# Eight row tiles normalised in four steps instead of two, and head 0 in another order

## What is computed

```python
xn = _layernorm(x, axis=-1)                      # mean, variance, eps 1e-5
x = x + _L0_attn_ref(xn, ...) + _L0_ffn_ref(xn, ...)

# attention: 16 heads of 128
q = rmsnorm(xn @ Wq, q_rms_w); k = rmsnorm(xn @ Wk, k_rms_w); v = xn @ Wv
scores = q @ k.T * scale + bias                  # bias = -distance * slope of the head
attn = softmax(where(causal, scores, -inf))
y = rmsnorm(attn @ v, subln_w)
out = y @ Wproj

# ffn: x / s rounded to float8, times s, then times the float8 weight * scale
```

## Time and profile before

| | |
|---|---|
| median of 3 runs | 524.42 us (524.07 to 524.53) |
| the profiled execution: time, span | 524.42 us, 522.5 us |
| TensorE (PE) busy | 508.9 us, 97% |
| VectorE (DVE) busy | 434.0 us, 83% |
| ScalarE (ACT) busy | 376.9 us, 72% |
| GpSimd (POOL) busy | 348.3 us, 67% |

### The profile page before, as it was taken

The page is one execution under the profiler, slowest core; times in us unless marked ns, Lnnn a source line. Parts: engine busy times, 40 slices in busy tenths (PEclk is TensorE's granted clock), DMA queues, the critical chain, the costliest instruction groups (busy, mean ns, idle before and its releaser), DMA issues. The chain is left out here.

```text
span 522.5 us, 11980 instructions
## 1 busy us (share of the span) xinstructions
PE 508.9 (97%) x3348; PEld 467.0 (89%) x3348; DVE 434.0 (83%) x1058; ACT 376.9 (72%) x887; POOL 348.3 (67%) x494
## 2 busy tenths in 40 slices
PE   8998999999999999999999999999999999999986
PEld 4987898999999899999989999998999999999775
DVE  5688789888888888898898888889888887988964
ACT  3678687687868768786776968678696867868650
POOL 5687885866858387783858658584885838667121
PEclk9999999999999999999999999999999999999999
DMA  5200101010010101001010000101000000000002
GB/s 156 72 2 11 31 1 41 3 32 10 2 41 0 40 0 40 0 0 40 0 40 0 21 19 0 40 0 40 0 14 26 0 10 0 11 1 1 3 0 80
DMA packets 18614, 10.82 MB, mean 21 GB/s; under 512 B 2208, under 2 KB 18592, under 8 KB 18592
## 3 DMA queue, kind: packets, MB, share of 16 engines
q1 hardware_dynamic: 17600, 10.49, 6.8%
q10 hardware_dynamic: 992, 0.07, 0.1%
HBM read 9.51 MB, written 1.05 MB: 20 GB/s over the span
## 5 line engine op out<-in xcount | busy, mean ns | idle before, releaser
L863 ACT ACTIVATE stage<-qkv_ps 128x384 f32<-128x384 f32 x116 | 57.1, 492 | 86.5 <-PE qkv_ps L551 86.5
L1110 DVE TENSOR_TENSOR pT_lo<-pT_ps,pT_hi 128x384 fp32r<-128x384 f32 (+2 forms) x192 | 100.6, 552 | 11.9 <-ACT pT_hi L891 11.7
L891 ACT ACTIVATE pT_hi<-pT_ps 128x384 fp32r<-128x384 f32 (+2 forms) x192 | 86.7, 485 | 28.9 <-PE pT_ps L634 28.8
L883 ACT ACTIVATE probs<-probs,neg_max 128x256 f32<-128x256 f32 (+7 forms) x128 | 99.0, 775 | 3.5 <-DVE neg_max L1101 2.7
L634 PE MATMUL pT_ps<-ident,probs 128*128 128x128 f32 x576 | 86.0, 276 | 4.2 <-ACT probs L883 2.9
L549 PE MATMUL qkv_ps<-w_hi,xT_hi 128*128 128x384 f32 x240 | 87.8, 366 | 0.0
L551 PE MATMUL qkv_ps<-w_hi,xT_lo 128*128 128x384 f32 x240 | 81.1, 338 | 0.0
L634 PEld LDWEIGHTS pT_ps<-ident,probs 128*128 128x128 f32 x576 | 66.2, 140 | 16.5 <-issue 5.8
L550 PE MATMUL qkv_ps<-w_lo,xT_hi 128*128 128x384 f32 x240 | 80.8, 336 | 0.0
L423 POOL TENSOR_TENSOR qk_r<-qk_ms,minus_half 128x4 f32<-128x4 f32 x64 | 64.9, 1015 | 17.1 <-DVE qk_ms L1077 15.7
L549 PE MATMUL yT_ps<-pT_hi,v_hi 128*128 128x256 f32 (+1 forms) x224 | 73.1, 326 | 0.4 <-DVE pT_lo L1110 0.4
(11 more groups left out here) (203 smaller groups left out, 1323.3 us busy)
## 6 DMA issues: line engine op xcount, KB each, us to landing
w_raw<-in_wq SPq DMA_DIRECT2D x16, 128.0 KB, 2.2
w_raw<-in_wk SPq DMA_DIRECT2D x16, 128.0 KB, 2.3
w_raw<-in_wv SPq DMA_DIRECT2D x16, 128.0 KB, 2.4
wp_raw<-in_wproj SPq DMA_DIRECT2D x16, 128.0 KB, 2.1
acc<-in_x SPq DMA_DIRECT2D x4, 256.0 KB, 4.9
out<-acc SPq DMA_DIRECT2D x8, 128.0 KB, 1.8
w<-in_ffn_w ACTq DMA_DIRECT2D x1, 64.0 KB, 5.7
q_col<-in_q_w ACTq DMA_DIRECT2D x1, 0.5 KB, 3.0
```

The costliest lines, as they stand in the source:

```text
L863: act.activation(stage_of(h, k // 2)[:, k % 2, :], qkv_bank(h, k)[:, 0:3 * D], ACT.Copy).then_inc(qkv_read, 1)
L883: act.activation(probs[:, s % 2, 0:(i + 1) * P], probs[:, s % 2, 0:(i + 1) * P], ACT.Exp, bias=neg_max[:, par, s:s + 1], scale=-1.0, accum ...
L891: act.activation(pT_hi[g][:, a:b, r * P:(r + 1) * P], pT_ps[(chunk0(h, s) + k) % 2][:, 0:(b - a) * P].rearrange("p (j t) -> p j t", t=P), ...
L1110: dve.tensor_tensor(pT_lo[g][:, a:b, r * P:(r + 1) * P], pT_ps[(chunk0(h, s) + k) % 2][:, 0:(b - a) * P].rearrange("p (j t) -> p j t", t=P ...
```

## The change

Loads: head 0's weights are loaded between the second and the third quarter of x. Prologue: moments, power and normalisation go by two row tiles, in four steps; row tiles 0 to 3 are normalised by ScalarE (`activation` with scale 1/std and a shift of -mean/std that VectorE computes, `shift_x`), row tiles 4 to 7 by VectorE as before. A PSUM bank of `xT_bank` now holds both halves of the channels of two tiles, so `round_xT` and `split_xT` do two whole row tiles each. The low part of head 0's weights is made in two pieces with a semaphore each. The warm-up has 16 products, and 2 behind each of the first two groups of transposes instead of 10 behind the first four tiles. Head 0: the same calls in another order on TensorE, ScalarE, VectorE and GpSimd. The FFN weights' transposes come before those of the last row tile. The number of bytes loaded and every product of the attention and the FFN are the same.

```diff
@@ on SP
-            for n in range(4):
+            def load_x(n):
                 quarter = slice(n * NT // 4, (n + 1) * NT // 4)
                 sp.dma_start(acc[:, quarter, :], x_v[:, quarter, :]).then_inc(x_loaded[n], 16)
...
+            load_x(0)
+            load_x(1)
             load_w(0, 0)
+            load_x(2)
+            load_x(3)
             load_w(1, 1)
             load_wp(0, 0)
@@ on GpSimd
-            for n in range(2):
-                at = slice(n * NT // 2, (n + 1) * NT // 2)
-                if n == 1:
-                    pool.wait_ge(w_hi_done, 1)
-                    pool.tensor_tensor(w_lo[:, 0], w_raw[:, 0], w_hi[:, 0].bitcast(f32), ALU.subtract).then_inc(w_split, 1)
+            def root_x(n):
+                at = slice(n * NT // 4, (n + 1) * NT // 4)
                 pool.wait_ge(var_ready, n + 1)
                 pool.tensor_tensor(rstd[:, at], rstd[:, at], minus_half[:, at], ALU.pow).then_inc(rstd_ready, 1)
+            def low_w(kt):
+                pool.wait_ge(w_hi_done, 1)
+                pool.tensor_tensor(w_lo[:, 0, kt], w_raw[:, 0, kt], w_hi[:, 0, kt].bitcast(f32),
+                                   ALU.subtract).then_inc(w_half if kt == 0 else w_split, 1)
...
-            pool.wait_ge(w_split, 1)
+            root_x(0)
+            root_x(1)
+            low_w(0)
+            low_w(1)
+            root_x(2)
+            root_x(3)
             pool.wait_ge(xn_ready, NT)
             split_w(1, 1)
             norm_qk(0, 0)
             norm_qk(0, 1)
             norm_qk(0, 2)
             norm_qk(0, 3)
+            norm_qk(1, 0)
             split_v(0, 0, 0)
             split_v(0, 0, 1)
-            norm_qk(1, 0)
             pool.wait_ge(small_loaded, 80)
             pool.wait_ge(xT_read, 2 * KT)
+            split_w(2, 0)
             split_v(0, 0, 2)
             split_v(0, 0, 3)
-            split_w(2, 0)
@@ on TensorE
-                    if isinstance(h, int) and h == 0 and k % 4 == 0:
-                        pe.wait_ge(xT_read, KT * (k // 4) + kt + 1)
+                    if isinstance(h, int) and h == 0 and kt == 0 and k % 2 == 0:
+                        pe.wait_ge(xT_read, k // 2 + 1)
+                    if isinstance(h, int) and (h, k) == (0, 0):
+                        pe.wait_ge(w_split if kt else w_half, 1)
...
             transpose_x(0)
-            warm(KEEP_WARM)
+            warm(2)
+            transpose_x(1)
+            warm(2)
             project(0, 0, 0)
             project(0, 0, 1)
-            transpose_x(1)
             project(0, 0, 2)
+            transpose_x(2)
+            transpose_x(3)
             project(0, 0, 3)
...
             project(0, 0, 7)
+            transpose_qk(0, 0, 0, -1)
             project(1, 1, 0)
-            transpose_qk(0, 0, 0, -1)
+            project(1, 1, 1)
             transpose_qk(0, 0, 1, -1)
-            project(1, 1, 1)
+            project(1, 1, 2)
             transpose_qk(0, 0, 2, -1)
             score(0, 0, 0)
             transpose_qk(0, 0, 3, -1)
-            project(1, 1, 2)
             project(1, 1, 3)
@@ on TensorE, first_head
                 transpose_probs(0, 0)
                 score(0, 0, 1)
                 project(1, 1, 4)
+                score(0, 0, 2)
                 project(1, 1, 5)
-                score(0, 0, 2)
+                project(1, 1, 6)
+                transpose_probs(0, 1)
                 score(0, 0, 3)
-                transpose_probs(0, 1)
-                project(1, 1, 6)
                 score(0, 0, 4)
                 transpose_probs(0, 2)
+                project(1, 1, 7)
+                transpose_probs(0, 3)
                 score(0, 0, 5)
-                transpose_probs(0, 3)
-                project(1, 1, 7)
                 transpose_qk(1, 1, 0, 0)
+                score(0, 0, 6)
                 transpose_probs(0, 4)
-                score(0, 0, 6)
                 score(0, 0, 7)
                 transpose_probs(0, 5)
                 transpose_qk(1, 1, 1, 0)
                 transpose_qk(1, 1, 2, 0)
                 attend(0, 0, 0, 0)
+                transpose_qk(1, 1, 3, 0)
                 transpose_probs(0, 6)
-                transpose_qk(1, 1, 3, 0)
                 attend(0, 0, 0, 1)
+                transpose_w8()
                 transpose_probs(0, 7)
                 score(1, 1, 0)
-                transpose_w8()
@@ on ScalarE
+            def normed(n):
+                act.wait_ge(shift_ready, n + 1)
+                for t in (2 * n, 2 * n + 1):
+                    act.activation(bias_xn(t), acc[:, t, :], ACT.Identity, scale=rstd[:, t:t + 1],
+                                   bias=x_shift[:, t:t + 1]).then_inc(xn_ready, 1)
...
+            normed(0)
+            round_w()
+            normed(1)
             round_xT(0)
             round_xT(1)
             act.wait_ge(const_ready, 3)
+            copy_qkv(0, 0)
             make_bias(0, 0)
-            copy_qkv(0, 0)
             copy_qkv(0, 1)
+            copy_qkv(0, 2)
             round_xT(2)
             round_xT(3)
-            copy_qkv(0, 2)
+            copy_qkv(0, 3)
             square_qk(0, 0)
-            copy_qkv(0, 3)
+            square_qk(0, 1)
             copy_qkv(0, 4)
...
@@ on VectorE
+            def shift_x(n):
+                at = slice(2 * n, 2 * n + 2)
+                dve.wait_ge(rstd_ready, n + 1)
+                dve.scalar_tensor_tensor(x_shift[:, at], mean_var[:, at, 0], -1.0, rstd[:, at],
+                                         ALU.mult, ALU.mult).then_inc(shift_ready, 1)
...
+            quarter_tables()
+            moments(0)
+            moments(1)
+            shift_x(0)
+            shift_x(1)
+            moments(2)
+            split_xT(0)
+            split_xT(1)
+            moments(3)
+            normed(2)
+            normed(3)
+            split_xT(2)
+            split_xT(3)
+            scale_q()
             mean_squares(0, 0)
...
             def first_head():
                 decode_w8(0)
+                probs_lo(0, 0)
+                mask(0, 0, 1)
                 decode_w8(1)
-                mask(0, 0, 1)
                 decode_w8(2)
-                decode_w8(3)
-                probs_lo(0, 0)
                 mean_squares(1, 1)
                 mask(0, 0, 2)
+                decode_w8(3)
+                decode_w8(4)
+                probs_lo(0, 1)
                 mask(0, 0, 3)
...
```

More of the change, by code:

```diff
@@ L162, in build_block @@
         w_split = sem("w_split")
+        w_half = sem("w_half")
+        shift_ready = sem("shift_ready")
         wp_split = sem("wp_split")
@@ L585, in project @@
             def project(h, par, k):
-                if k == 0:
+                if k == 0 and not (isinstance(h, int) and h == 0):
                     pe.wait_ge(w_split, h + 1)
@@ L700, in _, with transpose_x @@
             warm(WARM_UP)
-            def transpose_x(half):
-                for t in range(4):
-                    pe.wait_ge(xn_ready, 4 * half + t + 1)
+            def transpose_x(n):
+                for t in (2 * n, 2 * n + 1):
+                    pe.wait_ge(xn_ready, t + 1)
                     for kt in range(KT):
[L708 to L711, removed]
+                        last = pe.transpose(xT_bank(n)[:, (KT * kt + t % 2) * P:(KT * kt + t % 2 + 1) * P],
+                                            bias_xn(t)[:, kt * P:(kt + 1) * P], ident[:, :])
+                last.then_inc(xT_ready, 1)
             transpose_x(0)
-            warm(KEEP_WARM)
+            warm(2)
+            transpose_x(1)
+            warm(2)
             project(0, 0, 0)
             project(0, 0, 1)
-            transpose_x(1)
             project(0, 0, 2)
+            transpose_x(2)
+            transpose_x(3)
             project(0, 0, 3)
@@ L809, in head @@
                     if s in (2, 3, 4):
-                        if s == 4:
+                        if s == 4 and not first:
                             sum_y(h - 1, 1)
@@ L1160, in add_out, with tiles_of, moments, normed @@
                 last.then_inc(misc_read, 1)
-            def tiles_of(half):
-                return range(half * NT // 2, (half + 1) * NT // 2)
-            def moments(half):
-                for t in tiles_of(half):
-                    if t % 2 == 0:
-                        dve.wait_ge(x_loaded[t // 2], 16)
+            def tiles_of(n):
+                return range(n * NT // 4, (n + 1) * NT // 4)
+            def moments(n):
+                dve.wait_ge(x_loaded[n], 16)
+                for t in tiles_of(n):
                     last = dve.bn_stats(stats[:, t, :], acc[:, t, :])
                 link(last)
-            def variances(half):
-                for t in tiles_of(half):
+                for t in tiles_of(n):
                     last = dve.bn_aggr(mean_var[:, t, :], stats[:, t, :])
                 link(last)
-                at = slice(tiles_of(half)[0], tiles_of(half)[-1] + 1)
+                at = slice(tiles_of(n)[0], tiles_of(n)[-1] + 1)
```

(13 more changed lines are left out.)

85 lines of the change are left out of this document (36 added, 49 removed).

## The result

The changed kernel takes 527.46 us, median of seven executions from 525.49 to 529.09; the kernel before 524.42 (524.07 to 525.73). The ratio is 1.0048, 95% interval 1.0032 to 1.0064. The forecast was 522.5, range 521.0 to 524.8. The profiled execution is the fastest of the seven (525.49 us, span 523.5), so its trace explains 1.1 us of the 3.0; the rest is in the spread, which the kernel before had less of.

A forecast was written before the change was run, and what follows sets the result against it. TensorE, busy 508.9 of 522.5 us, was taken as the bound. Prologue 0.85 plus head 0 1.45, less 0.1 for x transposes and 0.35 for stretching, made 1.85: 524.4 to 522.5 us, range 521.0 to 524.8.

The forecast's parts named there:

- 0.85 forecast: Prologue: first projection near 11.7 instead of 12.52, 0.85 us won.
- I take a lead at that point to reach the end: First score of head 1 (52.66 before): TensorE is dense afterwards, so a lead there was to shorten the whole kernel equally.
- I leave the 1.9 us around it alone: Outside the span: 524.42 us of execution against a span of 522.5; this 1.9 us was taken as unchanged.
- Head 0, walked through with the durations of the rows ... 1.45 won: Head 0: TensorE's waits walked through in the new order, 3.2 us against 4.65 before, 1.45 won.
- row tile 7's score: Head 0: waits 0.35 us for the fourth q, k group's low part, starting at 28.25 instead of 29.54.
- weight copies and decode steps pass under two projections: Head 0, after row tile 7's score: these operations were to be covered by two projections, with no wait counted.
- I charge 0.35: Head 0: 0.35 us for one engine stretching another's operations, a few likely on the mask chain.
- The row of 0.70 us: Trace before: a 4-column VectorE operation that took 0.17 us once and 0.70 another time, 0.5 more.
- Rival D: Head 0: low parts behind masks and decode steps come 0.5 us late at eight row tiles, 526.2 us; chance 0.07.
- Rival B: Only the prologue pays; head 0's waits merely move and 4.65 us stays, 523.6 us; chance 0.19.
- Rival C: Prologue: TensorE's clock falls with too little work up to 11.7, costing 2.55 us more, 525.1 us; chance 0.10.
- the 0.3 apart that the prediction allows: Sign: wrong if the lead at head 1's first score differs from the lead at the end by over 0.3 us.

The follow-up runs named there:

- e14: Changed kernel with idle TensorE products in the prologue (3 and 6 instead of 2 and 2), head 0's two largest waits (4 and 5) and near the end: 525.59 us.
- e1: The changed kernel measured once more, no edit: 526.72 us.
- e15: New prologue with 3 and 6 products behind the transposes, head 0's lists as before the change, idle products near the end: 524.03 us.
- e16: Changed kernel with the edits of e7 and e8, plus idle products in the prologue, before head 0's fourth transposes and near the end: 524.09 us.
- e7: Changed kernel with GpSimd's split of head 2's weights moved back behind head 0's last two v splits: 528.25 us.
- e8: Changed kernel with VectorE's decode steps 3 and 4 behind row tile 6's mask instead of ahead of it: 528.49 us.
- e3: Changed kernel with 3 and 6 warm-up products behind the first two groups of transposes instead of 2 and 2: 526.68 us.
- e11: New prologue with head 0's lists as before the change, plus idle products near the end: 524.67 us.
- e17: Kernel before with 16 warm-up products instead of 24, 4 instead of 10 behind the transposes, and idle products near the end: 524.71 us.
- e10: Kernel before with three and two idle products in TensorE's two waits near the end: 524.46 us.
- e4: New prologue alone, with the lists of head 0 as before the change: 524.33 us.
- e13: Kernel before with only the loads in the new order: 524.55 us.

## Why the prediction was wrong

**The sum.** The changed kernel's 3.0 us are 1.2 to 1.3 of order, prologue included (e14 against the kernel before, 525.59 to 524.4 or 524.3), and about 1.9 of clock (527.46 to 525.59, and the same between the median spans, 525.6 and 523.7; against e1's median it is 1.1). The prediction had minus 1.85 and no clock. For head 0 alone e14 is to be held against e15, which has the same prologue and the old lists: the new lists cost 1.56 us (525.59 against 524.03) where the sum has 1.45 won.

**Prologue: right up to the first projection.** 0.85 forecast, 1.04 measured. ScalarE's two tiles took 1.09 us together, so 0.5 a step was right. The power over two columns took 0.71 and 0.70 instead of 1.02, and ScalarE had the second pair of tiles done at 9.77 instead of 10.4. Part of that was lost again: VectorE's two-column operation at 10.01 took 0.83 instead of 0.17 us and ended at 10.84, GpSimd's low parts ended at 10.82, and the split of x stands directly behind it. "I take a lead at that point to reach the end" and "I leave the 1.9 us around it alone" failed: with all falls away, e15 keeps 0.7 us of the lead in its span and 0.25 in its time.

**"Head 0, walked through with the durations of the rows ... 1.45 won": the step that failed.** The walk gave 3.2 us of waits, the trace has 6.5. Up to row tile 7's score (forecast 28.25, measured 28.59) it held within 0.35. Then "weight copies and decode steps pass under two projections" was taken as free: decode steps that take 0.42 us alone took 1.02, 1.94, 0.85 and 1.25, and the first three, ahead of row tile 6's mask, are 2.55 us too long. The mask came 2.7 us later than walked (35.7 against 38.43). There is a second part, which no long decode step explains. In e16, where the decode steps ahead of it take only 0.61 and 0.85 us, the mask still starts at 36.84, 1.1 us later than walked. It stands behind both pieces of row tile 7's low part there, and VectorE waited 1.04 us for their rounding (the 35.63 row); the kernel before has the mask ahead of them.

**"I charge 0.35" for one engine stretching another: mis-sized.** It was 2.55 us on the mask chain. The row of 0.70 us was read as chance. Its end, 23.59, is GpSimd's end (22.52 and 1.04 long, 23.56). It is a rule, not noise: a VectorE operation with one input, from SBUF, waits until GpSimd's is over. Its price is the rest of GpSimd's operation, here up to 1.5 us (1.94 against 0.42), and one was moved onto it. Five pairs of the rows above agree, four in the changed kernel and one in e7, with ends 0.27 to 0.29 us apart. The Trainium skill, "SBUF — State Buffer", section "SBUF: two separate sides", has a lock on a pair of ports that the two engines share: when the VectorE operation runs in a mode with two ports, or has two SBUF inputs and GpSimd's reads SBUF, whichever starts first holds the pair for the whole instruction, and the other fully blocks. The blocking agrees with the traces; the mode is in no row of them.

**Rival D** (VectorE's queue sets the end) is what came true of the span, by this mechanism and not by late low parts alone: with the decode steps and the split both moved, e16 has 1.5 us less than e14 (524.09 against 525.59; median spans 522.2 and 523.7). e7 and e8 each left the mask late, so neither edit alone does it.

**Rival B** (an order by hand only moves the waits) describes what was left: e16, with the new lists mended, and e15, with the old ones, take the same time (524.09 and 524.03). The 1.45 us of the walk appeared in no run.

**Rival C** (the clock falls) came true in another place. I looked for it in the prologue, where TensorE was idle 0.26 and 0.80 us; the trace of e3 has it after two waits of 1.07 and 1.33 us in head 0. I dismissed it because the steps after a wait of 0.58 us were still fast, and took no account that longer waits in head 0 would bring the same risk. Whether the prologue's holes count as well stays open: e11 against e15 speaks for it (4 of 12, none of 11), e17 against it (waits of 1.69 and 1.48 us there, no time lost in 11), and no profile shows a fall there. For the end it is e10 and the profile of e4. A fall costs 1.3 us in the kernel before (the medians of the 26 and the other 86 executions, 525.69 and 524.42) and 1.9 in e4: the clock is at 0.50 for three stretches of 1 us and parts of two.

**What would have warned.** The trace of the kernel before shows VectorE waiting for GpSimd in head 0 too, at a decode step (VectorE, then GpSimd):

```profile
...
32.46 0.42 DVE L1243 TENSOR_SCALAR y_sq<-y_sq 128x512 f32<-128x512 int32 x1
...
32.91 0.85 DVE L1245 TENSOR_SCALAR y_sq<-y_sq 128x512 int32<-128x512 int32 x1
...
```

```profile
...
32.74 0.73 POOL L442 TENSOR_TENSOR v_lo<-bias,v_hi 128x256 fp32r<-128x256 f32 x1
...
```

The step of 0.85 us ends at 33.76, GpSimd's operation at 33.47: 0.29 apart. And the kernel before falls too, in up to 26 of 112 executions; the three times shown at first happened to miss it.

**A sign that misled.** The first score of head 1 is 1.41 us later (54.07 against 52.66), the end of the span 1.0, more than the 0.3 apart that the prediction allows. No lead was won back: the FFN weights' transposes now stand ahead of that score, and at a later score of head 1, behind them in both kernels (59.81 against 58.71), the difference is 1.10.

**Open.** The time outside the span is 1.8 to 1.9 us in most executions of the kernel before, and 1.8 to 3.1 with the new prologue, 1.9 to 2.8 in e17, but 1.85 to 1.93 in all of e14 and e16. It isn't the order of the loads (e13). With fewer warm-up products it appears and with all places filled it goes, but e15, filled in two of three, still had it (up to 3.0). Its cause wasn't found; it eats a good part of what e15 wins in the span.

## What to carry to other kernels

Before a VectorE operation with one input in SBUF is moved, or a long GpSimd one, lay the two queues side by side: the price is what is left of the GpSimd operation, and it moves with each edit. A longer wait of TensorE costs itself and, in some executions, another 1.3 to 1.9 us by the clock; so look at the spread and the granted clock of several executions, not at one profile. Idle products placed inside waits that exist anyway cost nothing here (e14's spans are 523.3 to 524.2, the changed kernel's that lost nothing by the clock 523.1 to 524.4), and none of the 33 executions of e14 to e16 fell.

## What was not expected of the hardware

One profile can be undisturbed while more than half of the executions aren't: 525.49 us of 525.49 to 529.09. Five idle products of 0.21 us in the kernel before (e10) cut its range from 2.6 us to 0.4. Two edits that did not bring the mask forward one by one (e7 and e8: 38.51 and 38.22 against 38.43) brought it to 37.00 together and were worth 1.5 us.
